# Queries and keys of an attention layer turned by transposing DMAs instead of by TensorE and copies

## What is computed

```
x = x + (z @ R(cond) - z) @ U.T          # z = x @ U
for each of three layers:
    h = modulate(norm(x), shift, scale)
    q, k, v = split(h @ W_qkv + b)       # 16 heads of 9 channels; third layer: q, k normalised too
    attn = softmax(q k^T / sqrt(9))
    x = x + gate * ((attn @ v) @ W_proj + b)
    h = modulate(norm(x), shift, scale)
    x = x + gate * (gelu(h @ W_fc1 + b) @ W_fc2 + b)
```

## Time and profile before

| | us |
|---|---|
| median of 3 runs | 410.47 (409.33 to 413.35) |
| profiled execution | 414.15 |
| its span in the trace | 412.3 |
| from the end of the first parts of visit 0 to that of visit 23 | 243.5 |
| one pair of slots in the steady part (two visits, one MLP step) | 20.3 |

### The profile page before, as it was taken

One profiled execution on the slowest core, in us unless ns is written; L12 is line 12 of the kernel. 1 busy time (PEld: TensorE's weight loads), 2 busy tenths in 40 slices (PEclk: granted clock), 3 DMA queues, 4 the chain that ended last, 5 costly groups with the idle time before them and its releaser, 6 DMA issues.

```text
span 412.3 us, 11130 instructions
## 1 busy us (share of the span) xinstructions
PE 331.8 (80%) x3680; PEld 233.1 (57%) x3680; DVE 305.6 (74%) x1532; ACT 231.6 (56%) x506; POOL 165.8 (40%) x536
## 2 busy tenths in 40 slices
PE   2979449990265697999999999999998999898845
PEld 1827223580143465677777777776766666666634
DVE  5999987999934558578777777778988898976120
ACT  3253101142023356697979797878787868786721
POOL 5424312566331204344443435353645464533140
PEclk9997555577566669699999999999999999999978
DMA  5687000068000000000000000000000000000000
GB/s 149 190 260 230 0 1 3 0 136 290 1 2 0 2 2 2 2 2 2 2 2 2 2 2 2 2 3 2 2 2 2 2 2 2 3 16 2 16 14 14
DMA packets 10191, 14.14 MB, mean 34 GB/s; under 512 B 1770, under 2 KB 8654, under 8 KB 10008
## 3 DMA queue, kind: packets, MB, share of 16 engines
q1 hardware_dynamic: 10136, 13.45, 11.2%
HBM read 12.82 MB, written 0.62 MB: 33 GB/s over the span
## 4 chain that ended last, share of the span: by engine, by line
DVE 40%; PE 26%; issue 15%; ACT 9%; POOL 8%; DMA 0%; SPq 0%; POOLq 0%; ACTq 0%; DVEq 0%
PE ps L864 17%; DVE nmax L1645 5%; PE ps L1140 4%; DVE grow L1337 3%; DVE top L1392 3%; DVE trow L1337 3%; ACT skw_r L748 2%; DVE beta L1371 2%; ACT brief L709 2%; DVE den L1377 2%; PE ps L1197 2%; DVE tfac L1385 2%; DVE lead L1359 2%; ACT L740 2%; DVE st L1557 1%
## 5 line engine op out<-in xcount | busy, mean ns | idle before, releaser
L1645 DVE TENSOR_REDUCE nmax<-ps 128x4 f32<-128x512 f32 x96 | 62.6, 684 | 31.3 <-PE ps L864 31.2
L723 ACT ACTIVATE skw_t<-ps 128x512 f32<-128x512 f32 x96 | 53.4, 595 | 20.8 <-PE ps L864 20.5
L417 POOL TENSOR_TENSOR root<-grow,half 32x1 f32<-32x1 f32 x64 | 34.7, 542 | 56.6 <-DVE grow L1337 56.1
L864 PE MATMUL ps<-skw_r 54*128 54x128 bf16 x768 | 47.7, 222 | 5.8 <-DVE nmax L1645 4.0
L864 PEld LDWEIGHTS ps<-skw_r 54*128 54x128 bf16 x768 | 29.7, 96 | 27.1 <-issue 18.4
L533 POOL TENSOR_TENSOR rstd<-vare,nhalf 128x1 f32<-128x1 f32 x24 | 13.3, 553 | 69.6 <-DVE vare L1563 53.1
L864 PE MATMUL ps<-mT_t,fc1w_t 128*128 128x256 f32 x120 | 39.3, 420 | 1.4 <-ACT mT_t L761 1.3
L864 PE MATMUL ps<-fc2w,skw_r 128*128 128x144 f32 (+1 forms) x240 | 34.1, 290 | 0.6 <-ACT skw_r L748 0.6
L716 ACT ACTIVATE skw_r<-ps 128x512 bf16<-128x512 bf16 x48 | 26.1, 594 | 15.0 <-PE ps L1140 14.7
L1140 PE MATMUL ps<-identb,brief 128*128 128x128 bf16 x384 | 28.7, 234 | 5.2 <-DVE brief L1632 5.1
L864 PEld LDWEIGHTS ps<-fc2w,skw_r 128*128 128x128 f32 (+1 forms) x240 | 30.8, 190 | 2.0 <-ACT skw_r L748 1.0
(11 more groups left out here) (260 smaller groups left out, 839.4 us busy)
## 6 DMA issues: line engine op xcount, KB each, us to landing
gmod<-spread_mods SPq DMA_DIRECT2D x3, 1408.0 KB, 12.8
adaw_t<-in_ada SPq DMA_DIRECT2D x3, 432.0 KB
tails<-in_tail SPq DMA_DIRECT2D x3, 427.1 KB
skw_t<-in_skw SPq DMA_DIRECT2D x1, 1024.0 KB
fc1w_t<-in_fc SPq DMA_DIRECT2D x3, 320.0 KB
fc2w<-in_fc SPq DMA_DIRECT2D x3, 288.0 KB
qkvw_t<-in_qkv SPq DMA_DIRECT2D x3, 216.0 KB
x<-in_x SPq DMA_DIRECT2D x1, 576.0 KB, 6.2
```

The lines of the kernel that those rows point to most:

```text
L417: g.tensor_tensor(root[:, p, j:j + 1], grow[:, i % 4, 0:1], half[:], ALU.pow).then_inc(root_ready, 1)
L723: a.activation(prob[g].rearrange("p i t -> p (i t)"), ps[:, 2 + g % 2, :], ACT.Exp, scale=SCALE).then_inc(prob_ready, 1)
L864: return pe.matmul(o, lhsT, rhs, start=start, stop=stop, skip_group_check=True)
L1645: d.tensor_reduce(nmax[:, v % 2, first:first + 7:2], ps[:, 6 + g % 2, :].rearrange("p (i t) -> p i t", i=4), AX_X, ALU.max, negate=True).t ...
```

## The change

The sixteen transposes a visit on TensorE and the four copies (two on VectorE, two on ScalarE) are taken out. In their place SyncE's queue issues two transposing DMAs a visit, one for q and one for k, each from `parts[k][h]` (128 tokens by 1024 bf16 numbers) to `qkT[k][h]` (128 partitions by 8 blocks by 128 tokens). The queue waits for `parts_ready` and, from the third visit on, until the transposed scores of visit v - 2 are done, which read the buffer that is written now. `scores(v, 0)` waits for both DMAs to be complete. Every other instruction keeps its place.

```
-        qT_full, qT_ready = sem("qT_full"), sem("qT_ready")
-        kT_full, kT_ready = sem("kT_full"), sem("kT_ready")
+        q_turned, k_turned = [[sem(f"{n}_turned{h}") for h in range(2)] for n in "qk"]
...
+            for v in range(VISITS):
+                h = v % 2
+                sp.wait_ge(parts_ready, v + 1)
+                if v >= 2:
+                    sp.wait_ge(sT_full, 4 * (v - 2) + 4)
+                for k, turned in ((0, q_turned), (1, k_turned)):
+                    sp.dma_start_transpose(qkT[k][h], parts[k][h].rearrange("p h d -> p (h d)")).then_inc(turned[h], 16)
...
                 if v >= 2:
-                    act.wait_ge((qT_full, kT_full)[k], v - 1)
+                    act.wait_ge((q_turned, k_turned)[k][h], 16 * (v // 2))
...
-            def k_out(v):
...
-                    if new:
-                        k_out(v)
...
-            def parts_turn(v, k):
...
             def scores(v, g):
-                pe.wait_ge(qT_ready, 2 * v + g // 2 + 1)
-                pe.wait_ge(kT_ready, 2 * v + g // 2 + 1)
+                if g == 0:
+                    pe.wait_ge(q_turned[v % 2], 16 * (v // 2 + 1))
+                    pe.wait_ge(k_turned[v % 2], 16 * (v // 2 + 1))
...
-                if new:
-                    parts_turn(v, 0)
-                    parts_turn(v, 1)
...
-            def q_out(v):
...
-                    if new:
-                        q_out(v)
```

## The result

| | before | changed |
|---|---|---|
| median of the timed runs, us | 411.37 (4 runs) | 469.05 (467.02 to 475.94, 4 runs) |
| ratio of the two, 95% interval | | 1.139 (1.130 to 1.147) |
| profiled execution, span in the trace | 412.3 | 474.0 |

The change makes the kernel 57.7 us (14%) slower. The profiled execution is the longest of the four and in the slower state that some executions fall into, so the ratio leaves it out.

A forecast was written before the change was run, and what follows sets the result against it. TensorE's list was taken to bound the steady part, inside a closed ring. 414.15 us profiled + 98 for the ring + 36 for the clock = 548, or 544 us by the median (33% slower); range 418 to 655 us.

The forecast's parts named there:

- The closed ring: Scores need turned parts, maxima need scores, next parts follow the last maximum; DMA time beyond the 3.42 us gap counts fully.
- L = 7.5 us: Time from complete parts (`parts_ready`) to completion of both transposing DMAs of a visit, taken as the middle of two ends.
- lower end: Both DMAs complete 3.7 us after the parts, if a transpose costs what plain rows of 256 bytes cost.
- upper end: Both DMAs complete 11.3 us after the parts, if the writing side goes in pieces of 32 bytes.
- my fixed part: The part of a DMA's time from issue to landing that doesn't depend on size: 1.57 us, counted once a pair.
- The term for the ring: Loss over 24 hand-overs from parts to first scores: 24 x 7.5 - 82.2 = 98 us.
- The clock: TensorE's clock falls to half after idling about 5 us a visit: 1.5 us a visit, 36 us, ends 0 and 60.
- The rival of cheap transfers: Both DMAs complete 3.7 to 5 us after the parts, the clock holds: 417 to 455 us, chance 0.25.
- The possible gain of 25 us: With free DMAs, the gap from parts to scores shrinks by at most TensorE's 1.06 us of transposes, 24 times.
- the faster rival: TensorE's relief counts if both DMAs complete within 3.42 us of the parts: 386 to about 400 us, chance 0.03.
- The prices from the Trainium skill: Page figures for transposing DMAs: 1309 ns a 128x128 block, 21 us a visit one by one; elsewhere 350 to 400 GB/s.
- The queue's other duties: SyncE's four result stores stand behind the transposes, so early stores move back; claimed to cost nothing.

The follow-up runs named there:

- the second profile: The changed kernel, unaltered, run again for a second profiled execution: 464.02 us, ratio 1.125 to the kernel before; span in the trace 460.8 us.

## Why the prediction was wrong in size

The direction was right and its mechanism too; the size was not: 133 us forecast, 58 measured.

- **The closed ring: right.** The longer gaps show in full in every visit, a third DMA lengthened them by another 1.35 us each, and the loss disappears where the parts are made early enough.
- **L = 7.5 us: the step that failed.** It was the middle between a lower end from plain rows of 256 bytes (3.7) and an upper end from pieces of 32 bytes (11.3). Measured: 4.6 us typically, 4.8 to 5.0 in the mean with the late landings. The trace after shows packets of about 256 bytes, at 21.0 ns; so the small pieces on the writing side, on which the upper end rested, don't show. The lower end was 0.9 us short: an issue of 1.3 us where I took 0.38 of a plain load, and 21.0 instead of 16.5 ns a packet; in return the completion came quicker than my fixed part. The term for the ring, 98 us, became 33 to 38 in the two profiles. With 4.6 the same sum gives 24 x 4.6 - 82.2 = 28 us, and with the forecast clock term of 36 a time of 474.5 us, 5 above the result. That it comes so near is partly luck: late landings added 5 to 10 us to the ring, and the clock took 13 to 22 less than forecast. I should have weighed that a row of the right length stood in the trace, and none that spoke for small pieces.
- **The clock: right in kind, half as large.** Forecast 36 us (0 to 60), measured 14 and 23 us of longer ways in the two profiles; the run with the idle time filled brings the ways back to 164.4 us, against 163.8 before. With a gap of 4.6 us TensorE is idle in it for about 2 to 3 us instead of 5, and the clock falls in part of the visits only, as in the changed kernel's ways of 6.44 beside 8.98 us. The rival of cheap transfers had L right (3.7 to 5 us), and still its 455 us were passed, since it took the clock to hold when TensorE idles 1.3 to 2.6 us: in the second profile 13 of 23 ways have stretches at half clock, after gaps of 4.53 us too.
- **The possible gain of 25 us: wrong in the steady visits.** I took TensorE's share of 98% in the earlier trace rows for a bound and counted the 1.06 us of transposes as relief if the DMAs were fast. With plain DMAs that are complete in time the gaps stayed at 3.15 and 3.5 us in visits 5 to 14. VectorE's `attended` and GpSimd's tail end at the same time as TensorE's list; the transposes lay in that shadow. There the faster rival was worth nothing, whatever L; only at half clock, in the first visits, did the relief show, and for the odd visits of the third layer no run tells.
- **The prices from the Trainium skill.** The 1309 ns for a 128x128 block (VectorE: DVE Perf Modes, "The three transpose paths") is near the 1.3 us that eight blocks took here, so it isn't a price that adds up over blocks. The 350 to 400 GB/s of Advanced Engine Details and Errata, "X-Bar Transpose (TRN2)", were not reached: 256 KB in 1.3 to 1.4 us are some 200 GB/s, and the issue of 1.3 us caps the queue at the same rate. Nor were the transposes as fast as plain DMAs here: the plain copies of the same 256 KB ran at 330 to 420 GB/s.
- **The queue's other duties** cost nothing that shows; the stores stayed at the end.

What is open: how the loads of instructions hold the transfers up, and which ways the low clock strikes. A layout in which one DMA carries the first half of both queries and keys, so that two issues serve both halves, wasn't tried.

## What to carry to other kernels

Before moving work from a busy engine to DMA, find the ring: if the transfer's result is needed by work whose outcome starts the next transfer, its latency counts in full each time round, and the number to compare is the gap that exists now, not the busy time saved. Two transposing DMAs in one queue cost their two issues of 1.3 us, whether they move 128 or 256 KB, so put fewer and larger ones, and give them work made one step ahead. A DMA in the ring also meets whatever else uses the DMA engines, the loads of the program's own instructions here. And a bound at 98% busy may have others lying just behind it: replacing the work by something that is surely in time, such as a plain copy, tells in one run what its removal is worth, in the visits where it is indeed in time.

## What the runs showed of the hardware

- A transposing DMA from SBUF to SBUF takes 1.2 to 1.3 us of SyncE's queue for its issue, for 128 KB (1268 ns) as for 256 KB (1320 ns); a plain DMA of the same 256 KB took 550 ns.
- 256 KB were turned and complete 3.0 us after the issue began when alone, and 3.3 in a pair; 128 KB 2.5 us; a plain copy of 256 KB 2.4 us.
- While they ran, the transposes moved 200 to 230 GB/s (packets of some 256 bytes, 21.0 ns each) and the plain copies 330 to 420 GB/s.
- Most landings agree within 0.2 us, but some took up to 5.5 us; the plain copies had one of 3.7 too. Pairs of transposes with no load of instructions in flight were complete 4.41 to 4.56 us after the first issue (53 visits of five profiles), those with one after 4.41 to 6.32 us (67 visits).
- After waits with 2 to 3 us of idle time TensorE's granted clock fell to 0.50 in part of the visits; a way of 6.44 us at full clock took 7.99 us with a mean of 0.79.
